# Latent attention: weighted sums of two batches together behind scores, three of four output products in the next pair's round

## What is computed

```python
q_hk = (hidden_q @ Wq.T).reshape(Bv, Sv, H, K)
q_big = jnp.einsum('bshk,hkq->bshq', q_hk, w_kc_q)
...
q_big = _apply_rope(q_big, sin_q[None, :, None, :], cos_q[None, :, None, :])
...
kv_r = _apply_rope(kv_c, sin_k[None], cos_k[None])
q_r = jnp.einsum('bshq,hqr->bhsr', q_big, W_qr)
k_r = jnp.einsum('bld,hdr->bhlr', kv_r, W_kr)
scores = jnp.einsum('bhsr,bhlr->bhsl', q_r, k_r)
attn = jax.nn.softmax(scores, axis=-1)
ctx_c = jnp.einsum('bhsl,bld->bhsd', attn, kv_r)
ctx_lat = jnp.einsum('bhsd,hkd->bhsk', ctx_c, w_kc_kv)
ctx = ctx_lat.transpose(0, 2, 1, 3).reshape(Bv, Sv, H * K)
return ctx @ Wo.T
```

## Time and profile before

| what | value |
|---|---|
| median of 3 runs | 1368.71 us |
| lowest and highest | 1364.29, 1371.57 us |
| profiled execution: span | 1363.2 us |
| median less that span | 5.5 us |
| TensorE busy in the span | 1232.2 us (90%) |
| VectorE busy | 813.6 us (60%) |
| ScalarE busy | 559.4 us (41%) |
| GpSimd busy | 522.7 us (38%) |
| stage of the change, first queries to last outputs | 848.64 to 1114.9 us |

### The profile page before, as it was taken

One profiled execution on the slowest core, in us unless ns is written; L12 is line 12 of the kernel. 1 busy time (PEld: TensorE's weight loads), 2 busy tenths in 40 slices (PEclk: granted clock), 3 DMA queues, 4 the chain that ended last, 5 costly groups with the idle time before them and its releaser, 6 DMA issues. The chain is left out here.

```text
span 1363.2 us, 25223 instructions
## 1 busy us (share of the span) xinstructions
PE 1232.2 (90%) x9232; PEld 785.4 (58%) x9232; DVE 813.6 (60%) x1828; ACT 559.4 (41%) x1333; POOL 522.7 (38%) x595
## 2 busy tenths in 40 slices
PE   7999999949786787999999977999999989999998
PEld 4969687736445344566665664455555554444487
DVE  5474646558345476676876525777777773734253
ACT  4544647244123566777777432234444441000010
POOL 3543626550661367476677302422222211600010
PEclk9999999959798888999999867999999999999999
DMA  3010119454786201212222210100003006642000
GB/s 135 25 38 0 38 33 337 138 227 180 220 254 207 82 12 22 47 30 40 38 33 34 26 39 21 47 22 22 22 22 90 2 1 194 183 142 70 23 9 24
DMA packets 144169, 106.60 MB, mean 78 GB/s; under 512 B 87872, under 2 KB 130088, under 8 KB 142912
## 3 DMA queue, kind: packets, MB, share of 16 engines
q1 hardware_dynamic: 135360, 88.24, 22.6%
q0 software_dynamic: 4496, 13.33, 3.5%
q10 hardware_dynamic: 4208, 3.61, 0.9%
HBM read 84.16 MB, written 22.35 MB: 78 GB/s over the span
## 5 line engine op out<-in xcount | busy, mean ns | idle before, releaser
L2965 PE MATMUL la_banks<-la_xe,la_f_w 128*128 128x512 f32 x348 | 153.1, 598 | 3.6 <-DVE la_xe L3343 3.6
L2316 DVE SCALAR_TENSOR_TENSOR dh_front<-dh_pj,df_conv,dh_front 128x510 f32<-128x510 f32 x144 | 107.4, 746 | 63.3 <-ACT dh_front L2010 59.6
L3506 POOL TENSOR_TENSOR la_area<-la_area 128x512 f32<-128x512 f32 x48 | 60.4, 1280 | 172.4 <-DVE la_area L3186 152.1
L2965 PEld LDWEIGHTS la_banks<-la_xe,la_f_w 128*128 128x128 f32 x348 | 66.0, 192 | 84.8 <-issue 84.8
L353 POOL TENSOR_TENSOR wa_qkT<-lf_area 128x512 f32<-128x512 f32 x40 | 50.9, 1271 | 97.3 <-DVE lf_area L325 97.3
L3343 DVE TENSOR_TENSOR la_xe<-xT,la_area 128x1024 f32<-128x1024 f32 x29 | 52.7, 1833 | 56.5 <-PE la_banks L2965 49.8
L3083 ACT ACTIVATE la_area<-la_banks,la_nmax 128x256 f32<-128x256 f32 x128 | 59.0, 475 | 58.6 <-DVE la_nmax L3195 58.6
L357 POOL TENSOR_TENSOR mw_gu<-mw_gu,const 128x384 f32<-128x384 f32 x64 | 63.7, 1000 | 29.9 <-ACT mw_gu L388 29.9
L3526 POOL TENSOR_TENSOR la_o_rstd<-la_o_var,la_minus_half 128x1 f32<-128x1 f32 x8 | 6.4, 805 | 166.0 <-DVE la_o_var L3405 166.0
L3091 ACT COPY la_area<-la_banks 128x512 f32<-128x512 f32 x64 | 37.5, 590 | 56.2 <-PE la_banks L2814 55.9
L280 PE MATMUL wa_po<-wa_wo,mw_rows 128*128 128x256 f32 x256 | 56.6, 379 | 0.0
(11 more groups left out here) (640 smaller groups left out, 3011.7 us busy)
## 6 DMA issues: line engine op xcount, KB each, us to landing
mw_gu<-in_L_ffn_gate_up SPq DMA_DIRECT2D x16, 768.0 KB, 16.4
placed<-mw_rows SPq DMA_DIRECT2D x8, 768.0 KB, 11.7
mw_d<-in_L_ffn_down SPq DMA_DIRECT2D x16, 384.0 KB, 16.8
mw_rows<-placed SPq DMA_DIRECT2D x8, 768.0 KB, 6.5
la_area<-w_table POOLq DMA_DIRECT2D x6, 1024.0 KB, 11.6
pairs<-me_picked SPq DMA_DIRECT2D x7, 704.0 KB, 3.8
la_f_w<-in_L_ffn_q_proj SPq DMA_DIRECT2D x32, 128.0 KB, 2.2
la_f_w<-in_L_ffn_k_proj SPq DMA_DIRECT2D x32, 128.0 KB, 2.5
```

Of the source, the lines that this page charges most:

```text
L2316: dve.scalar_tensor_tensor(dst, src[:, :, 0:SEQ - j], conv[:, a, m, D_CONV - 1 - j:D_CONV - j], dst, ALU.mult, ALU.add).then_inc(tapped, 1)
L2965: mm = pe.matmul(acc[c][m], f_w[n % SLOTS][:, m, k, :], xe[(n - U) % RING][:, k, :], start=first and k == 0, stop=last and k == KC - 1)
L3506: pool.tensor_tensor(qrot[:, c, n, :], prod[:, c, 2 * n, :], prod[:, c, 2 * n + 1, :], ALU.add).then_inc(rotated, 1)
```

## The change

Only the order of calls changes; every instruction is there as before. On TensorE `outputs(j, 1)`, `(j, 2)` and `(j, 3)` are issued in the next round, each behind a block of `queries` or a `turn`; `attend` of batches 0 and 1 stand together behind `scores(j, 3)` and a turn, those of batches 2 and 3 together behind `scores(i, 0)`; the turns of batches 2 and 3 stand around the two `latent_queries`. ScalarE and VectorE follow with their copies, adds and norms. In the tail `outputs(LAST - 1, 1)` and the adds of batches 0 and 1 of the pair before the last come in.

```diff
--- before.py
+++ after.py
@@ -2850,45 +2850,47 @@
                     j = i - 1
                     queries(i, 0, 0)
                     queries(i, 0, 1)
+                    if j >= 1:
+                        outputs(j - 1, 1)
                     if j >= 0:
                         scores(j, 1)
+                    queries(i, 0, 2)
                     if j >= 1:
                         outputs(j - 1, 2)
-                    queries(i, 0, 2)
                     queries(i, 1, 0)
                     if j >= 0:
                         turn(j, 0, 0)
+                    queries(i, 1, 1)
+                    if j >= 0:
                         scores(j, 2)
                         turn(j, 0, 1)
-                    queries(i, 1, 1)
+                    if j >= 1:
+                        outputs(j - 1, 3)
+                    queries(i, 1, 2)
                     if j >= 0:
                         turn(j, 1, 0)
-                    if j >= 1:
-                        outputs(j - 1, 3)
-                    if j >= 0:
-                        attend(j, 0)
-                    queries(i, 1, 2)
-                    if j >= 0:
                         scores(j, 3)
                         turn(j, 1, 1)
+                        attend(j, 0)
                     if i == 0:
                         sim_norms()
-                    latent_queries(i, 0)
                     if j >= 0:
                         attend(j, 1)
                         turn(j, 2, 0)
+                    latent_queries(i, 0)
+                    if j >= 0:
+                        turn(j, 2, 1)
+                        turn(j, 3, 0)
                     latent_queries(i, 1)
                     if j >= 0:
-                        turn(j, 2, 1)
+                        turn(j, 3, 1)
                     scores(i, 0)
                     if j >= 0:
-                        turn(j, 3, 0)
+                        attend(j, 2)
+                        attend(j, 3)
                         outputs(j, 0)
-                        turn(j, 3, 1)
-                        attend(j, 2)
-                        outputs(j, 1)
-                        attend(j, 3)
                 scores(LAST, 1)
+                outputs(LAST - 1, 1)
                 scores(LAST, 2)
                 outputs(LAST - 1, 2)
                 turn(LAST, 0, 0)
@@ -3102,15 +3104,14 @@
                         exp(j, 2)
                         copy_eT(j, 1, 0)
                         copy_eT(j, 1, 1)
+                        exp(j, 3)
+                        copy_eT(j, 2, 0)
+                        copy_eT(j, 2, 1)
                     copy_qc(i, 0)
                     if j >= 0:
-                        exp(j, 3)
-                        copy_eT(j, 2, 0)
-                    copy_qc(i, 1)
-                    if j >= 0:
-                        copy_eT(j, 2, 1)
                         copy_eT(j, 3, 0)
                         copy_eT(j, 3, 1)
+                    copy_qc(i, 1)
                     exp(i, 0)
                 exp(LAST, 1)
                 copy_eT(LAST, 0, 0)
@@ -3242,39 +3243,41 @@
 
                 for i in range(PAIRS):
                     j = i - 1
+                    if j >= 1:
+                        add(j - 1, 0)
                     if j >= 0:
                         norm(j, 0)
                     rope(i, 0, 0)
+                    rope(i, 0, 1)
                     if j >= 0:
                         maximum(j, 1)
-                    rope(i, 0, 1)
+                    if j >= 1:
+                        add(j - 1, 1)
                     rope(i, 0, 2)
                     if j >= 1:
                         add(j - 1, 2)
                     if j >= 0:
                         norm(j, 1)
                         maximum(j, 2)
+                    rope(i, 1, 0)
+                    rope(i, 1, 1)
+                    if j >= 0:
+                        norm(j, 2)
+                    if i == 2:
+                        sim_scaled()
                     if i == 0:
                         sim_squares()
-                    rope(i, 1, 0)
-                    rope(i, 1, 1)
+                        sim_bound()
                     if j >= 1:
                         add(j - 1, 3)
                     if j >= 0:
-                        norm(j, 2)
-                    if i == 0:
-                        sim_bound()
-                    elif i == 2:
-                        sim_scaled()
+                        maximum(j, 3)
                     rope(i, 1, 2)
                     if j >= 0:
-                        maximum(j, 3)
                         copy_cx(j, 0)
                         norm(j, 3)
                     maximum(i, 0)
                     if j >= 0:
-                        add(j, 0)
-                        add(j, 1)
                         copy_cx(j, 1)
 
                 def x_stats(t):
@@ -3408,8 +3411,10 @@
                     dve.wait_ge(o_rstd_ready, t + 1)
                     dve.tensor_scalar(env.x[:, t, :], env.x[:, t, :], o_mv[:, t, 0:1], o_rstd[:, t:t + 1], ALU.subtract, ALU.mult).then_inc(o_normed, 1)
 
+                add(LAST - 1, 0)
                 maximum(LAST, 1)
                 norm(LAST, 0)
+                add(LAST - 1, 1)
                 maximum(LAST, 2)
                 add(LAST - 1, 2)
                 norm(LAST, 1)
```

## The result

| what | before | after |
|---|---|---|
| median of the runs taken together (4 each) | 1367.81 us | 1380.16 us |
| lowest, highest | 1364.29, 1371.57 us | 1376.78, 1386.95 us |
| profiled execution: span | 1363.2 us | 1378.1 us |
| the stage, first queries to last outputs | 266.3 us | 280.2 us |

The changed kernel is slower by 1.0%: ratio 1.0103, 95% interval 1.0080 to 1.0126. The forecast was 1378.2 us. The stage alone grew by 13.9 us; the profiled span grew by 14.9 us, of which 1.0 us lies ahead of the stage (it begins at 849.62 us, 848.64 before), where nothing is changed.

A forecast was written before the change was run, and what follows sets the result against it. TensorE's full list bounds the 32.20 us steady round; a cheaper list with a new wait adds 1.29 us, 7.7 over six. With third round 0.6 and tail 1.2, +9.5 us: 1368.7 becomes 1378.2 us, range 1369 to 1385.

The forecast's parts named there:

- The list: TensorE's instructions in a steady round: the new order leaves scores or attend less often, 31.31 us, 0.89 less than now.
- the new entry of `attend` behind `scores`: TensorE, two attend straight behind scores: extra between 0 and 0.2 us, taken as 0.
- The wait in the middle: TensorE ahead of turn(j,3,0), which needs norm(j,3) from VectorE: a wait of 2.18 us, all paid.
- the string: VectorE's work from the end of scores(j,2) through norm(j,3): 12.95 us, against 10.77 us of TensorE's middle.
- the two turns on one bank: turn(j,2,1) and turn(j,3,0) share a bank: the second waits 0.59 us for ScalarE's copy, covered by norm(j,3).
- rival A: VectorE: norm(j,2) not held by GpSimd, string 11.00 us, round about 32.05 us, total 1369.6 us; chance 0.15.
- First half: ... Sum 13.06 us: TensorE from the round's start through scores(j,2): pieces sum to 13.06 us, with VectorE through in time.
- End: turn(j,3,0) 0.44: TensorE from turn(j,3,0) to outputs(j,0): that turn priced at 0.44 us in a sum of 7.48 us.
- the tail: After the rounds, add(6,1) and outputs(6,2) stand ahead of the last pair's first turns: 0.6 to 1.5 us, taken as 1.2.
- The third round's 0.6 us: Third round: three small gate instructions (0.59 us) move from slack into the string, costing 0.6 us.
- B: TensorE's list alone counts, all waits hidden: 6 x -0.89 + 1.8 = -3.5, total 1365.2 us; chance 0.03.
- C: VectorE: copy_cx also held by GpSimd's third add, +0.92 us a round, total 1383.7 us; chance 0.10.

The follow-up runs named there:

- the last experiment: Kernel before, calls reordered so TensorE never waits (outputs moved, scores(j,2) in its old place, attend between the latent_queries): steady round 31.51 us against 32.20, ratio 1.0001.
- two of the variants above: Changed kernel with add(k,1) ahead of maximum(j,1), 1377.56 us; changed kernel with add(k,3) ahead of norm(j,2), 1379.89 us.
- the control: Kernel before, with GpSimd's first two adds of the second half made to wait for norm(j,2): steady round 32.20 us as before, one run 1360.66 us.

## Why the prediction was right

**The list.** Right: the pieces kept their prices, the new entry of `attend` behind `scores` costs 0, and in the last experiment a list in which nothing waits is shorter by the amount that the pieces give, 0.69 us. The changed order itself was never seen without waits, so its own 0.89 rests on the same pieces.

**The wait in the middle.** Right in place, releaser and length: from the end of scores(j,2) to turn(j,3,0) 13.0 us were measured (984.74 to 997.75), 12.95 forecast. Of TensorE's idle time 0.76 us falls ahead of turn(j,2,1) already, for a copy that the prediction had near 24.2 us, and 1.13 ahead of turn(j,3,0); the string is no longer for it. norm(j,2) took 3.18 us in every steady round and norm(j,3) 1.44, as priced. That the hold is one cause and the late scores(j,2) the other is shown: either taken away alone gives 32.65 us. What lies under the wait was named rightly, the two turns on one bank, but not its size: rival A had 32.05 us for it. Of the 0.6 us between, 0.34 are the wait of outputs(k,2), and 0.2 the turn that starts behind a wait (0.63 us in place of 0.44).

**What was mis-sized.** The stage grew by 13.9 us, not 9.5, and a steady round took 34.12 us, above the 33.3 to 33.8 that was to show the forecast right. The first term is the step "First half: ... Sum 13.06 us", which has no wait ahead of outputs(k,2). That call waits for add(k,1), which stands behind maximum(j,1). By the prediction's own durations the add ends at 5.35 + 1.14 + 0.60 = 7.09 us of the round, 0.17 us ahead of its use at 7.26. It ended at 7.23 (978.54), and outputs(k,2) started at 7.37: the hand-overs that were left out as some hundredths each used up the margin. This cost 0.34 us a round, 2 us over six, as putting the add ahead showed. The second is the step "End: turn(j,3,0) 0.44": behind a wait this turn takes 0.65 us, 0.2 us a round, 1.3 us over six. The third, the tail, taken as 1.2, measured 1.6 (22.04 against 20.44 us), just above the upper end of 1.5: the first turns start 5.3 us into it in place of 3.7, behind the second output product. What is left, some 0.7 us, is under 0.1 us a round, most of it hand-overs in the string, and the first two rounds, which were taken as unchanged and took 0.17 and 0.08 us more. The third round's 0.6 us was measured as 0.60.

**What was luck.** The median came within 2 us of the forecast, nearer than its parts: the profiled span was 1378.1 us, 5.4 above the 1372.7 forecast, and the stage 4.4 us longer than forecast. The four runs of a kernel spread over 7 to 10 us, so the nearness of the median is in part chance. Two figures of the prediction also don't follow from its terms: the tail's ends and 0.2 us a round for `attend` give 1377.6 to 1379.7 us, not 1374 to 1382, and by its own shares the chance of "within 0.5%" is 0.28, not 0.24.

**The rivals.** A fell: norm(j,2) was held in every round. B fell: TensorE idled. C fell: copy_cx began 0.05 us ahead of GpSimd's add and took its 0.69 us; the case in which the add begins first was not seen. The clock, which the prediction took to cost nothing, was 1.00 from the second round to the tail of the profiled execution; two of the variants above show that a fall behind such waits can cost 1.7 us.

## What to carry to other kernels

A list made cheaper on the engine that is always busy is a gain only if each producer keeps its lead: before moving calls closer together, add up the string of the next engine between the two calls, with its durations as they are beside its neighbours and not alone. Here a price that was free under a full list (a held norm, in the control) became 1.5 us a round when the list left 13 us of VectorE's work only 10.8 us of cover. A wait ahead of such a string counted in full here, and more than its own length: 0.10 us of idle time made the round 0.34 us longer. So a margin of 0.1 or 0.2 us between two engines is none until the hand-overs are counted.

## What had not been expected of the hardware

A group of four transposes that starts behind a wait takes 0.65 us where it takes 0.44 in a running list, and outputs behind a wait of 0.10 us takes 1.10 us in place of 0.86: in these rows a stop on TensorE costs some 0.2 us beyond its own length, about as much as leaving `scores` or `attend`. The length of the round agrees: without the wait of 0.10 us it is 0.34 us shorter.
